# Two block boundaries removed, waits moved and a rounding step given to ScalarE in a two-layer attention and feed-forward kernel

## The reference, cut to what matters

```
x = x + attention0(norm(x), ctx, ctx)            # here called the mixing: 8 heads per 256 x 512 block, softmax over 512
x = x + rms_normed(down(silu(gate(n)) * up(n)))  # 4-bit weights, scales per group of 128; n = norm(x), 1408 wide
x = x + attention1(norm(x), ctx)                 # 16 heads of 32, 2048 queries by 2048 keys, all rounded to 8 bits
x = x + w2q @ gelu(w1q @ norm(x) + b1) + b2      # ternary weights, 2048 wide
```

## Time and profile before

| | us |
|---|---|
| median of three executions | 1841.76 (1841.43 to 1841.95) |
| the profiled execution | 1840.47 |
| its span in the profile | 1838.7 |
| TensorE busy | 1692.4, 92% of the span |
| VectorE busy | 1500.0, 82% |
| ScalarE busy | 1249.5, 68% |
| GpSimd busy | 907.8, 49% |
| mixing, to TensorE's last instruction in it | 0 to 350 |
| gated feed-forward, TensorE | 360 to 686 |
| keys, values, queries, TensorE | 686 to 895 |
| attention, ScalarE's exponentials | 905 to 1538 |
| projection and ternary feed-forward | 1538 to 1835 |

### The profile page before, as it was taken

How to read it: one execution, slowest core, us unless ns; L and a number is a source line. 1 busy time by engine, 2 the same in 40 slices (tenths; PEclk the granted TensorE clock), 3 DMA queues, 4 the chain that set the end, 5 groups by cost and what they waited for, 6 DMA issues and landing times.

```text
span 1838.7 us, 30262 instructions
## 1 busy us (share of the span) xinstructions
PE 1692.4 (92%) x10553; PEld 746.9 (41%) x10706; DVE 1500.0 (82%) x2800; ACT 1249.5 (68%) x2107; POOL 907.8 (49%) x927
## 2 busy tenths in 40 slices
PE   3999999779999998889899999999999998999999
PEld 1333323224444443334344444444444444444444
DVE  5899999877767666887799999999999997883332
ACT  4888888445554441223499999999999996774333
POOL 5667666346445430000188888888888885000000
PEclk9999999889999999999899999999999999999999
DMA  9855651211011005456566666766666668111120
GB/s 208 226 145 135 156 135 41 69 49 23 1 23 56 8 1 157 89 103 117 101 110 108 107 109 108 112 113 113 115 112 108 109 105 244 26 24 32 38 46 23
DMA packets 420631, 170.45 MB, mean 93 GB/s; under 512 B 382080, under 2 KB 391296, under 8 KB 419328
## 3 DMA queue, kind: packets, MB, share of 16 engines
q1 hardware_dynamic: 420480, 168.51, 44.3%
HBM read 69.89 MB, written 4.19 MB: 40 GB/s over the span
## 4 chain that ended last, share of the span: by engine, by line
PE 54%; DVE 14%; ACT 5%; issue 4%; POOL 3%; DMA 1%; DVEq 0%; POOLq 0%; SPq 0%; ACTq 0%
PE a_psM L1501 10%; PE g_psY L1043 7%; PE g_psG L1030 7%; PE a_psS L1549 7%; PE t_psD L2015 6%; DVE maxima L1515 6%; PE t_psU L2002 5%; PE a_psO L1561 3%; PE k_psA L1419 3%; ACT a_prob L1637 3%; POOL a_wide L1617 2%; PE k_psA L1390 2%; PE k_psA L1401 2%; PE t_psD L1726 1%; ACT g_sum L978 1%
## 5 line engine op out<-in xcount | busy, mean ns | idle before, releaser
L1515 DVE TENSOR_REDUCE maxima<-a_psM 128x1 f32<-128x512 f32 x1024 | 623.7, 681 | 7.5 <-PE a_psM L1501 5.9
L1637 ACT ACTIVATE a_prob<-a_psS,maxima,q_scale 128x1024 uint8<-128x1024 f32 x512 | 611.0, 1208 | 22.7 <-PE a_psS L1549 14.8
L1617 POOL CAST a_wide<-a_pairs 128x2048 int16<-128x2048 uint8 x256 | 483.2, 1898 | 98.6 <-DMA a_pairs<-a_prob 83.6
L1501 PE MATMUL a_psM<-KT,QO 128*128 128x512 bf16 x968 | 350.8, 385 | 15.2 <-DVE maxima L1515 10.5
L1549 PE MATMUL a_psS<-KT,QO 128*128 128x512 bf16 x966 | 294.5, 382 | 10.6 <-ACT a_prob L1637 7.7
L1561 PEld LDWEIGHTS a_psO<-V,a_wide 128*128 128x128 f16 x4096 | 175.3, 96 | 141.0 <-DVE QO L1590 23.0
L880 DVE SCALAR_TENSOR_TENSOR g_sum<-g_psG,gu_scale,g_sum 128x512 f32<-128x512 f32 x176 | 124.2, 746 | 89.9 <-PE g_psG L1030 75.1
L1561 PE MATMUL a_psO<-V,a_wide 128*128 128x32 bf16 x4096 | 181.3, 177 | 16.9 <-DVE QO L1590 15.6
L859 POOL TENSOR_TENSOR g_sum<-g_sum 128x512 f32<-128x512 f32 x88 | 126.6, 1438 | 140.3 <-DVE g_sum L880 140.3
L518 ACT ACTIVATE prob<-psT 128x512 f32<-128x512 f32 x256 | 143.1, 599 | 63.6 <-remote 32.0
L978 ACT ACTIVATE g_sum<-g_psG,gu_scale 128x512 f32<-128x512 f32 x176 | 111.4, 682 | 109.6 <-PE g_psG L1030 108.8
(11 more groups left out here) (219 smaller groups left out, 2736.4 us busy)
## 6 DMA issues: line engine op xcount, KB each, us to landing
xs<-in_x SPq DMA_DIRECT2D x64, 256.0 KB, 6.2
cs<-in_ctx SPq DMA_DIRECT2D x64, 256.0 KB, 8.3
KT<-in_w SPq DMA_DIRECT2D x2, 4096.0 KB, 19.2
raw_gu<-in_gu SPq DMA_DIRECT2D x4, 1408.0 KB, 8.1
vs<-in_ctxT SPq DMA_DIRECT2D x16, 256.0 KB, 2.8
a_pairs<-a_prob SPq DMA_TRANSPOSE x256, 3.0
out<-x_sb SPq DMA_DIRECT2D x16, 256.0 KB, 2.9
x_sb<-in_x SPq DMA_DIRECT2D x1, 3584.0 KB, 13.3
```

The costliest lines, as they stand in the source:

```text
L1501: pe.matmul(psM[n % NM][:, :], QOf[:, i * P:(i + 1) * P], KTf[:, keys:keys + 512], start=True, stop=True).then_inc(shown, 1)
L1515: v.reduce_max(tops[i // JOIN % NB][:, i % JOIN, c:c + 1], psM[n % NM][:, :], AX.X).then_inc(topped, 1)
L1617: pool.tensor_copy(wide[i % NV][:, :, :, :].rearrange("p k c q -> p k (c q)"), both).then_inc(widened, 1)
L1637: act.activation(prob[i % NP][:, k * HK:(k + 1) * HK], psS[g % NS][:, :], ACT.Exp, scale=q_scale[:, i:i + 1], bias=bias[i // JOIN % NB][:, ...
```

## The change

- `constants` and `mix_rows` return their five functions and stand at the head of the one block. The semaphores of the constants are waited for where they are used. GpSimd makes the bf16 identity first.
- The last tile's four reciprocals and the two last `after` leave the mixing. `gated_ffn` calls them in VectorE's order at t = 0: two reciprocals behind each fold of m = 0, one `after` behind each fold of m = 2.
- `normaliser` at t = 0 is cut in two: the 16 aggregations at p = 3, the inverse roots at p = 4 (both were at p = 1).
- In mixing steps with j < 0 all four statistics stand behind `maxima_rows`.
- SP's waits for `rows` and `taken` are moved behind its transfers of the value bias, context groups 1 and 2 and the key weights; only `products` stays ahead of them.
- The subtraction into `vq` is done by ScalarE (`whole`), behind the copies of k3, k4, k11 and k12.
- `normaliser` (behind v7) and `bias_rows(1)` (behind v5) both stand behind v1.
- GpSimd's `offset(0)` and `offset(1)` stand ahead of its wait for the turned queries.
- `less_round` is set at the start of the keys stage.

```diff
 def mix_rows ... gated_ffn
-                    if n in STATS and has(j + 3):
+                    if n in STATS and has(j + 3) and j >= 0:
                         statistics(j + 3, STATS.index(n))
...
-                if has(j + 3):
-                    statistics(j + 3, 2)
-                    statistics(j + 3, 3)
+                for h in range(0 if j < 0 else 2, HT if has(j + 3) else 0):
+                    statistics(j + 3, h)
...
-            for h in range(HT):
-                invert(NT - 1, h)
-            after(NT - 2)
-            after(NT - 1)
-            v.wait_ge(after_s, NT)
...
+        def last_tile(v, step):
+
+            if step < HT:
+                invert(v, NT - 1, step)
+            if step == HT:
+                after(v, NT - 2)
+            if step == HT + 1:
+                after(v, NT - 1)
+                v.wait_ge(after_s, NT)
...
                     for i in SIDES:
                         fold(m, i)
+                        if m == 0:
+                            last_tile(v, 2 * i)
+                            last_tile(v, 2 * i + 1)
+                        if m == 2:
+                            last_tile(v, 4 + i)
...
                         unpack_down(p)
-                        if p == 1:
-                            normaliser(v, env)
+                        if p == 3:
+                            aggregate(v, env, 0, NT)
+                        if p == 4:
+                            invert_roots(v, env, 0, NT)
...
 def keys_values_queries, sync
-            for done in ("products", "rows", "taken"):
-                sp.wait_ge(*env["ffn_done"][done])
+            sp.wait_ge(*env["ffn_done"]["products"])
             sp.dma_start(bv[:, :], bv_in).then_inc(loaded[1], 16)
             fetch_ctx(1, 2)
             sp.dma_start(wkv[:, :, 0:DM], wkv_in[:, 0:DM].rearrange("(c p) n -> p c n", p=P)).then_inc(loaded[7], 16)
             fetch_ctx(2, 3)
+            sp.wait_ge(*env["ffn_done"]["rows"])
+            sp.wait_ge(*env["ffn_done"]["taken"])
             sp.dma_start(raw[1][:, :], bq_in.partition_broadcast(P)).then_inc(loaded[6], 16)
...
 scalar
+            def whole(c):
+                act.wait_ge(v_own, 4 * (c + 1))
+                if c:
+                    act.wait_ge(v_turned, 16 * c)
+                act.activation(vq[:, :].rearrange("p (c k m) -> p c k m", k=2, m=P),
+                               vT[c % 2].rearrange("p (c m k) -> p c k m", k=2, m=P), ACT.Identity,
+                               bias=less_round[:, :]).then_inc(v_ready, 1)
...
                     keys(i)
+                    if i + AHEAD - 1 in LAST:
+                        whole(LAST.index(i + AHEAD - 1))
...
 vector, quantise
                 own.link(v.tensor_scalar(vT[c % 2], vT[c % 2], v_inv[:, at], ROUND, ALU.mult, ALU.add))
-                if c:
-                    v.wait_ge(v_turned, 16 * c)
-                v.tensor_scalar(vq[:, :].rearrange("p (c k m) -> p c k m", k=2, m=P),
-                                vT[c % 2].rearrange("p (c m k) -> p c k m", k=2, m=P), ROUND, None,
-                                ALU.subtract).then_inc(v_ready, 1)
...
-                    if i == 5:
+                    if i == 1:
+                        v.wait_ge(*env["ffn_done"]["stats"])
+                        normaliser(v, env)
                         v.wait_ge(b_own, 5)
                         bias_rows(1)
                         v.wait_ge(b_own, 10)
-                    if i == 7:
-                        v.wait_ge(*env["ffn_done"]["stats"])
-                        normaliser(v, env)
...
 attend, gpsimd
+            offset(0)
+            offset(1)
             for b in range(2):
                 pool.wait_ge(env["keys_done"]["turned"][b], 16 * NT)
-            offset(0)
-            offset(1)
```

More of the change, by code:

```diff
@@ L104, in normalise_tiles @@
     env["norm_count"] += own.n
+def normalise_tiles(v, env, first, end):
+    aggregate(v, env, first, end)
+    invert_roots(v, env, first, end)
 def normaliser(v, env):
@@ L472, in _, with scalar @@
             finish(NT - 1)
-        @block.scalar
-        def _(act):
+        def scalar(act):
             def roots(j):
```

147 lines of the change are left out of this document (78 added, 69 removed).

## The result

The changed kernel takes 1810.49 us, median of four (1809.8 to 1810.69), against 1841.6 for the kernel before in the same session (1840.79 to 1841.95): a ratio of 0.9834, 95% interval 0.9822 to 0.9846. The forecast was 1810.7. The profiled execution took 1810.41 with a span of 1808.6, 30.1 us less than before.

What follows compares the result with a forecast made beforehand. TensorE, busy 92% of the span, was taken to set the pace most of the time; 2.5 + 3.6 + 8.1 + (8.6 - 1.3) + 4.3 + 5.3 = 31.1 us off 1840.47 gave 1809.4, 1810.7 as a median; range 1806 to 1815.

Steps and rivals of the forecast that it cites:

- Start: At the start, x issued 2.55 us earlier brings the first statistics 2.55 earlier; gain 2.5 (2 to 2.6).
- Step j = -1: In mixing step j = -1, twelve maxima start at once, two moved statistics give back 0.6; gain 3.6 (0 to 4.2).
- End of mixing: At the boundary to the feed-forward, its start follows the second transpose at 353.0 instead of 360.50: 7.4 us earlier.
- Between the folds: Early feed-forward: moved reciprocals give back 1.5 us (1.0 to 2.7), two statistics at m = 2 give back 0.7.
- Keys stage: First wait and slow restart go, 8.6 us less 1.3 given back; second wait gains 4.3 (1 to 7.8).
- The subtraction: Keys stage: ScalarE takes 2.1 us against VectorE's 1.23; the skill's strict reading would cut the sum by about 3 us.
- Attention: At the head of attention, ScalarE's first exponential starts 5.3 us earlier (3.5 to 6).
- rival 4: In attention, a changed rhythm makes ScalarE wait 0.2 us in each of 256 heads, costing 51 us: 1862; chance 0.04.
- 1 (transfers take back a part of the front): Early work and transposes or keys context: transfers give back 3.6 and 3 us: 1817; chance 0.12.
- 3 (gaps close better in keys and attention): Boundary keeps the higher clock, worth 1.8 us; the keys' second wait gives 7.8 instead of 4.3: 1805; chance 0.12.
- rival 2: At m = 0, p = 4, k0 and the keys' second wait, moved work comes back, 9.2 us: 1820; chance 0.12.
- rival 5: At the feed-forward's start, the merged block does nothing; 8.1 and 2.5 us fall away: 1821; chance 0.05.

Runs made afterwards that it cites:

- x ahead of gamma: The changed kernel with x's first four transfers issued ahead of gamma's; 1807.61 us, ratio 0.9826.
- the two blocks: The changed kernel with mixing and the rest in separate blocks, the last tile's reciprocals and statistics at mixing's end again; 1812.96 us, ratio 0.9849.
- the normaliser at p = 1: The changed kernel with the two last statistics at m = 1 and all aggregations and inverse roots at p = 1 again; 1812.47 us, ratio 0.9845.
- SP's waits alone: The changed kernel with SP's waits for rows and taken back ahead of its keys-stage transfers; 1814.33 us, ratio 0.9856.
- The run: The changed kernel with the subtraction into vq back on VectorE and none on ScalarE; 1808.39 us, ratio 0.9825.
- the kernel with all down steps later: The changed kernel with x before gamma, reciprocals before the first fold, subtraction on VectorE, and value_down and scale_down one m later; 1804.44 us, ratio 0.9811.
- three together: The changed kernel with x issued before gamma, the last tile's reciprocals before the first fold, and the subtraction back on VectorE; 1805.75 us, ratio 0.9814.
- the statistics in the kernel before: The kernel before with only all four statistics behind the maxima in mixing steps with j under 0; 1837.05 us, ratio 0.9991.

## Why the forecast came out right

- **Start, 2.5 forecast, 1.18 measured.** The issue moved by the 2.5; the step that failed is "so they come 2.55 earlier", which took the transfer's duration as fixed. It took 7.59 us instead of 6.53. Gamma's transfer beside it is at least about half of that (x ahead of gamma).
- **Step j = -1, 3.6, measured 2.40** (2.1 to 3.1 in three comparisons). The wait is gone whole. What I left out is that VectorE, without it, is paced by sixteen maxima in a row, and reaches the split when GpSimd is at work: CAST and TENSOR_TENSOR take 0.41 and 1.07 instead of 0.18 and 0.17. The whole of four statistics then stands ahead of tile 1's maxima, not half covered.
- **End of mixing, 7.4 for the start, 6.31 measured.** The difference, 1.1, is the second transpose: 5.0 instead of 3.9, a duration again taken over from before. By the forecast's own sign, TensorE waiting longer than 4 us at the boundary, this term was wrong: it waits 4.09.
- **Between the folds.** The forecast gave 1.5 + 0.7 for reciprocals and statistics; the two blocks show 3.3, with 2.1 to 4.8 possible. So it isn't shown that this term was too small: the inside of the feed-forward gave 1.1 less than forecast, and 0.8 of that is what the profiled execution lies above the usual. The forecast expected the stretched unpacking only as a possible 0.94; it came (1.37). The Trainium skill, page SBUF — State Buffer, section Who interferes with whom, has the later of the two instructions stand until the earlier is through; the trace agrees. Of the 22 unpacking instructions on the down weights after, the 12 with no GpSimd tensor_tensor beside them took 0.43 to 0.47 us, 9 with one beside them 1.37 to 1.50 (each ending 0.28 us behind GpSimd's), and one that had started before GpSimd's 0.39. Before it was the same, 11 and 10, with one between; I had read it off the mask alone, and the shift ahead of it was stretched nine times in eleven.
- **Normaliser, 3.4 less 0.5: agrees** (2.9, the normaliser at p = 1; its own spread is that of the usual, some 1.5 either way).
- **Keys stage, 7.3 + 4.3 forecast, 13.48 measured.** The first wait and its give-back came as reckoned: v2 without a gap, 0.91 at v5 and 1.2 given back for 1.3. The second was mis-sized: 5.6 (shift at v8 17.08, at v10 22.71) instead of 4.3, because TensorE loses 2.2 us around v9 and k6, with waits of 0.24 and 1.46, and not 3.5. The two edits cover for each other: SP's waits alone are worth 6.3, not 8.8.
- **The subtraction.** I weighed the Trainium skill's rule (page Perfetto Trace Analysis, section Optimizing Scalar/DVE Operations) that VectorE is the quicker where it has a fast mode and that handing work over may pay where VectorE is saturated, priced it at 3 us, and left it out of the sum. The run decides for the rule's sign: 1.2 us are lost by the move. Its full price of four times 0.9 did not come, since the move shows only where TensorE is near a wait, at v9 and k6. The duration of 2.1 was forecast to the tenth.
- **Attention, 5.3, measured 5.3 at the first exponential** (904.86 less 876.21, less the 23.35 by which the scores were earlier) and 0.9 more behind it, which I had not counted: before, TensorE stood 4.32 us behind its first scores, and from 905.0 to 911.8 us its granted clock was 0.50; after, it does not stand there, and the clock is 1.00 from 877.7 us on. The rhythm of a head did not change: the rest is 922.39 and 922.95, so rival 4 is out.
- Of the rivals, 1 (transfers take back a part of the front) and 3 (gaps close better in keys and attention) both came in part, 3.6 us too little at start, step j = -1 and transpose (2.4 of it by transfers, 1.2 by VectorE at j = -1), 2.8 too much in keys and attention, and with 1.1 less inside the feed-forward and 1.0 more in queries and rest they cancelled but for 1.0. That they did is luck. Of rival 2 at most the give-back at m = 0 came, and rival 5 did not: the merged block does hold, by 6.3 us.

## What to carry to other kernels

When a wait goes, don't take the duration of what ends last next from the old row: what is issued earlier runs beside other things (x beside gamma, the split beside GpSimd), and a duration can change without a new neighbour, as that of the transposes did. Two waits on the same chain cover for each other, so that each alone is worth less than it shows. And look at what stands queued behind a waiting instruction on its engine: three things that need not stand there (four reciprocals, value_down, the subtraction) and two loads in the other order were worth another 8.8 us.

## What was not expected of the hardware

**Transposes by DMA differ with where their buffers lie, or so it looks; this was not tried.** In the changed kernel and the eleven made from it the transposes of the feed-forward took longer than in the two with the old layout. The view of the transfers, kernel before:

```profile
g_xT_hi<-g_half_hi SPq DMA_TRANSPOSE x2, 3.7
g_xT_lo<-g_half_lo SPq DMA_TRANSPOSE x2, 4.0
first_xT_hi<-qs SPq DMA_TRANSPOSE x1, 3.9
```

The kernel after:

```profile
g_xT_hi<-g_half_hi SPq DMA_TRANSPOSE x2, 4.3
g_xT_lo<-g_half_lo SPq DMA_TRANSPOSE x2, 5.1
first_xT_hi<-qs SPq DMA_TRANSPOSE x1, 4.4
```

The packets themselves are slower: each pair of transposes moves 4096 of 256 bytes before and after, and one takes, on average, 18 to 19 ns in the two old kernels and 21 to 22 ns in the other twelve. Two blocks did not bring it back, nor did other neighbours in time. One thing that all twelve share, among the rest of the change, is `less_round`, now set up ahead of the feed-forward's memory: it takes 32 bytes, and the buffers that these transposes read and write moved from multiples of 512 bytes (first_xT_hi at 74240, and xs0 behind it at 82432) to 32 beyond (74272 and 82464). The keys stage's transposes of the same size speak for the multiple and against the move as such: their buffers moved by the same 32 bytes but lay off a multiple of 512 before too, and they took the same in both:

```profile
KT<-k_parts SPq DMA_TRANSPOSE x16, 4.3
```

A kernel with `less_round` set up elsewhere would tell; it was not run, and the cause stays open.

**Mixing has a second, slower rhythm.** In the profiled execution of the kernel with all down steps later, the rows of maxima (mrow) came every 20.94 us for seven steps:

```profile
132.15 0.66 DVE L655 TENSOR_TENSOR mrow<-psS,of_block 51x512 bf16<-51x512 bf16 x1
153.08 0.66 DVE L655 TENSOR_TENSOR mrow<-psS,of_block 51x512 bf16<-51x512 bf16 x1
174.02 0.66 DVE L655 TENSOR_TENSOR mrow<-psS,of_block 51x512 bf16<-51x512 bf16 x1
```

In three together, with the same code there, every 19.83:

```profile
131.29 0.66 DVE L655 TENSOR_TENSOR mrow<-psS,of_block 51x512 bf16<-51x512 bf16 x1
151.12 0.66 DVE L655 TENSOR_TENSOR mrow<-psS,of_block 51x512 bf16<-51x512 bf16 x1
170.94 0.66 DVE L655 TENSOR_TENSOR mrow<-psS,of_block 51x512 bf16<-51x512 bf16 x1
```

It cost that execution 7.6 us (it took 1810.72; the other three of the same kernel 1801.96 to 1805.49), and the profiled one of the statistics in the kernel before 3.3. What starts it is open. With the 2.7 us by which the first columns of the feed-forward differ along with the length of the low clock, it is why totals here scatter by more than most of the edits are worth, and why the stretches decide.
